# A hand-written table of steps for the work beside a state-space scan, in a fused block of scan, mixture-of-experts and attention on one Trainium2 core

## What is computed

```python
x = x + ssm(layernorm(x))        # stage 0 of the kernel, the one that the change touches
x = x + ffn(layernorm(x))        # shared experts: beside the scan; 64 routed experts: stage 1
x = x + attention(layernorm(x))  # stage 2
x = x + ffn(layernorm(x))        # stage 3

def ssm(x):                      # per batch; 16 states, rank 128
    dt_raw, b, c = split(x @ W_x.T)
    dt = softplus(dt_raw @ W_dt.T + b_dt)
    h[t] = exp(dt[t] * a) * h[t-1] + dt[t] * b[t] * x[t]     # a = -exp(A_log)
    return sum_over_states(h * c) + x * D_param

def ffn(x):
    scores = softmax(x @ gate_w.T)                 # 64 experts, the best 6, at most 64 tokens each
    y = routed experts, silu(x @ w_gate) * (x @ w_up) @ w_down, weighted by the scores
    return y + silu(x @ sw_gate) * (x @ sw_up) @ sw_down      # the shared experts
```

## Time and profile before

| | us |
|---|---|
| median of three runs | 3288.41 |
| the profiled execution, its own time | 3294.18 |
| its span | 3292.4 |
| scan stage, first to last step | 38.6 to 1144.9 |
| tail, to the first expert's work | 1145 to 1216 |
| routed experts, attention, second feed-forward | from 1216 |

### The profile page before, as it was taken

How to read it: one execution, slowest core, us unless ns; L and a number is a source line. 1 busy time by engine, 2 the same in 40 slices (tenths; PEclk the granted TensorE clock), 3 DMA queues, 4 the chain that set the end, 5 groups by cost and what they waited for, 6 DMA issues and landing times.

```text
span 3292.4 us, 38105 instructions
## 1 busy us (share of the span) xinstructions
PE 2838.2 (86%) x13772; PEld 1516.4 (46%) x13772; DVE 1785.2 (54%) x3715; ACT 1281.2 (39%) x2673; POOL 1542.7 (47%) x949
## 2 busy tenths in 40 slices
PE   4668888778888879888868999999799899999998
PEld 2445545544555434333335555555444443444443
DVE  5898897989889942212235666665324344222221
ACT  4556566555656511101116666667412121011111
POOL 6998798978879802121226555555200000212212
PEclk7669999988999989999979999999899999999999
DMA  5443453535345369999930000000234220899997
GB/s 183 141 164 129 161 187 122 191 108 191 134 161 174 134 226 339 346 344 345 330 118 1 27 27 27 27 14 14 103 112 146 93 74 21 292 350 331 345 347 196
DMA packets 199053, 557.67 MB, mean 169 GB/s; under 512 B 25040, under 2 KB 26960, under 8 KB 198352
## 3 DMA queue, kind: packets, MB, share of 16 engines
q1 hardware_dynamic: 181168, 514.19, 44.9%
q0 software_dynamic: 16640, 39.86, 5.4%
q10 hardware_dynamic: 1056, 1.18, 0.1%
HBM read 480.42 MB, written 74.74 MB: 169 GB/s over the span
## 4 chain that ended last, share of the span: by engine, by line
PE 55%; DVE 13%; POOL 12%; DMA 8%; ACT 5%; issue 4%; SPq 3%; POOLq 0%; DVEq 0%; ACTq 0%
PE bank L976 9%; PE bank L1037 7%; PE bank L943 6%; PE bank L964 6%; POOL arena L1717 6%; DMA arena<-in_w_up 4%; PE bank L1084 4%; PE bank L1141 3%; POOL arena L1723 3%; PE bank L1063 3%; PE bank L1118 3%; DVE arena L1222 3%; DVE bank L1222 2%; PE bank L885 2%; PE bank L915 2%
## 5 line engine op out<-in xcount | busy, mean ns | idle before, releaser
L1717 POOL TENSOR_TENSOR arena<-arena 128x1024 f32<-128x1024 f32 x256 | 613.2, 2396 | 90.6 <-PE bank L915 77.9
L1575 ACT ACTIVATE bank<-arena 128x512 f32<-128x512 f32 x512 | 344.1, 687 | 409.5 <-DVE arena L1222 295.5
L915 PE MATMUL bank<-arena 128*128 128x128 f32 x2048 | 308.4, 303 | 181.4 <-POOL arena L1723 181.0
L1806 POOL TENSOR_TENSOR arena<-arena 128x2048 f32<-128x2048 f32 (+3 forms) x128 | 296.8, 2321 | 277.8 <-DVE arena L1443 277.8
L915 PEld LDWEIGHTS bank<-arena 128*128 128x128 f32 x2048 | 260.2, 156 | 264.6 <-POOL arena L1723 216.0
L976 PE MATMUL bank<-arena 128*128 128x512 f32 (+1 forms) x768 | 360.5, 613 | 15.1 <-DVE arena L1245 15.1
L1638 ACT ACTIVATE arena<-arena 128x256 f32<-128x256 f32 (+3 forms) x512 | 286.2, 562 | 201.7 <-DVE arena L1434 171.5
L1222 DVE TENSOR_TENSOR_SCAN arena<-bank,arena 128x512 f32<-128x512 f32 x256 | 311.1, 1215 | 67.8 <-ACT bank L1575 45.4
L1723 POOL TENSOR_TENSOR arena<-arena 128x512 f32<-128x512 f32 x256 | 326.8, 1277 | 33.6 <-DVE arena L1222 32.9
L1037 PE MATMUL bank<-arena 128*64 128x352 f32 x2048 | 328.6, 475 | 0.0
L1222 DVE TENSOR_TENSOR_SCAN bank<-bank,arena 128x512 f32<-128x512 f32 x256 | 308.5, 1205 | 0.0
(11 more groups left out here) (134 smaller groups left out, 4196.0 us busy)
## 6 DMA issues: line engine op xcount, KB each, us to landing
arena<-scratch_bc SPq DMA_DIRECT2D x128, 1024.0 KB, 5.4
arena<-in_w_gate SPq DMA_DIRECT2D x128, 704.0 KB
arena<-in_w_up SPq DMA_DIRECT2D x128, 704.0 KB
arena<-in_w_down SPq DMA_DIRECT2D x128, 512.0 KB
arena<-in_w_down SPq DMA_DIRECT2D x128, 192.0 KB
scratch_x<-arena SPq DMA_DIRECT2D x16, 1024.0 KB, 4.5
scratch_xn<-arena SPq DMA_DIRECT2D x15, 1024.0 KB, 8.6
arena<-scratch_x SPq DMA_DIRECT2D x48, 256.0 KB, 5.9
```

What stands on the lines that cost most here:

```text
L915: i = nc.tensor.matmul(y[:, t * P:(t + 1) * P], w[:, n, t * P:(t + 1) * P], p.ident, is_transpose=True, start=False, stop=g == GROUPS - 1 ...
L1575: nc.scalar.activation(bank[p.da_bank(k, n)][:, :], block_of(p.dt, b, c), ACT.Exp, scale=p.alog[:, c, state:state + 1]).then_inc(*p.decaye ...
L1717: nc.gpsimd.tensor_tensor(out=p.hb[k % HB], in0=over(block_of(p.dtx, b, c), 1, NG), in1=p.bc[k // 2 % NBC][:, 0], op=ALU.mult).then_inc(*p ...
L1806: nc.gpsimd.tensor_tensor(out=own, in0=own, in1=over(p.rden[:, k % 2, :], 2, width), op=ALU.mult).then_inc(*p.divided.up(k))
```

## The change

`scan_plan` no longer draws pieces from generators. A table names, for each kind of thing, the step in which it stands, counted from the start of the batch beside which it begins; `prepare_track`, `quad_track` and `first_track` put the things into a list for each step. Within a step the things that take a product off its bank (`TAKERS`) come first. `route1` is cut in two, `route1` and `masks`, two steps apart. `stats` is cut in two pieces, two tiles each; for the preparation they stand in steps 7 and 8, for the front both in step 1. Picks run on into the next batch (steps 33 to 41 are 1 to 9 of it). The tail has a new table (`MADE_BESIDE`, `TAKEN_BESIDE`). No instruction's size changes; the shared experts of quad 6 end in the tail, and quad 7 begins only in stage 1, where before its first two chunks stood at the tail's end.

```diff
+PREPARE = (("x_in", 4), ("stats_a", 7), ("stats", 8), ("rstd", 8), ("apply", 11))
+FRONT = (("stats_a", 1), ("stats", 1), ("rstd", 1), ("apply", 3), ("xn_out", 3), ("gate", 7), ("logit", 9), ("route_max", 10), ("route_exp", 12), ("route1", 13), ("masks", 15))
...
+GATES, UPS = (23, 26, 29, 30, 32, 35), (23, 26, 29, 30, 33, 35)
+DOWNS = (40, 41, 43, 51)
+TURN_LAG, DT_LAG, SILU_LAG, HID_LAG, SO_LAG = 1, 2, 2, 2, 2
...
+MADE_BESIDE = {"stats": 2, "logit": 1, "pick0": 1, "pick4": 1, "merge": 1, "lists": 1}
+TAKEN_BESIDE = {"rstd": ("silu",), "apply": ("hid",), "route_exp": ("silu",), "masks": ("hid",), "pick4": ("so",),
+                "merge": ("so",), "lists": ("so",)}
...
+def quad_track(q):
+
+    f = ("F", 0, q)
+    for name, at in FRONT:
+        yield at, ((name, f) if name in ("stats_a", "stats", "rstd", "apply") else (name, 0, q))
...
+    for j in range(SC):
+        yield GATES[j], ("sg", 0, q, j)
+        yield UPS[j], ("su", 0, q, j)
+        yield GATES[j] + SILU_LAG, ("silu", 0, q, j)
+        yield UPS[j] + HID_LAG, ("hid", 0, q, j)
+    for t in range(QT):
+        yield DOWNS[t], ("fetch", 0, q, t)
+        yield DOWNS[t], ("sd", 0, q, t)
+        yield DOWNS[t] + SO_LAG, ("so", 0, q, t)
...
+TAKERS = ("turned", "dtr_out", "bc_out", "dt_out", "logit", "folded", "silu", "hid", "so")
...
-        if k <= NSTEP:
-            plan += next(coming, [])
+        if k < NSTEP:
+            plan += sorted(beside[k], key=lambda i: i[0] not in TAKERS)
         if 0 < k <= NSTEP:
-            more = next(beside, [])
-            plan += more
...
+            plan += [("sum", k - 1)]
...
-        if name == "logit":
-            plan += own[2:]
...
+        for kind in TAKEN_BESIDE.get(name, ()):
+            plan += [i for i in pending if i[0] == kind]
+            pending = [i for i in pending if i[0] != kind]
+        if name == "pick4":
+            plan += own[OUT:]
...
+    def stats_a(n):
+        sums(n, range(QT // 2))
...
     def route1(m, q):
...
         nc.vector.memset(f["top"][:, :, TOPK:], -1.0).then_inc(*p.routed.up(m, q, "six"))
+
+    def masks(m, q):
+        f, s = p.ff[m], q % 2
+        score, marked = f["score"][s], f["marked"]
         V.wait_ge(p.routed, m, q, "six")
```

More of the change, by code:

```diff
@@ L310, in scan_plan @@
                 plan += [("bc_in", k // 2 + NBC - 1)]
[L311 to L314 removed]
+        if k >= X1_BEHIND:
+            b0, c0, g0 = step_of(k - X1_BEHIND)
             if g0 == GROUPS - 1:
                 plan += [("x1", b0, c0)]
[L317 to L323 removed]
@@ new lines, in scan_plan @@
+        if 0 < k <= NSTEP:
+            plan += [("sum", k - 1)]
+    left = [i for items in beside[NSTEP:] for i in items]
+    pending = [i for i in left if i[0] in ("silu", "hid", "so") and (*PRODUCT[i[0]], *i[1:]) in plan]
+    products = [i for i in left if i[0] in ("sg", "su", "sd")]
+    own = [i for i in left if i[0] == "fetch"]
+    weights = ([("w_up", 0, e), ("w_down", 0, e)] for e in range(RING_W[0]))
+    chain = itertools.chain(front_steps(0, BATCH - 1), route_steps(0, BATCH - 1),
+                            [[("merge", 0)], [("lists", 0), ("turnover", 0)] + [("gather", 0, n) for n in range(RING_X[0])]])
@@ L354, in scan_plan @@
+    plan += own[:OUT]
+    for more in chain:
         plan += more
@@ L424, in front_plan @@
         plan += units.spend(early[0])
-        plan += [("route1", m, q)]
+        plan += [("route1", m, q), ("masks", m, q)]
         for step in coming[3:]:
@@ L1174, in stats @@
             V.wait_ge(p.xt_in[n[2] % 2], n[1], n[2])
-        for t in range(QT):
+        for t in tiles:
             if n == ("S", 0):
```

192 lines of the change are left out of this document (73 added, 119 removed).

## The result

The changed kernel takes **3191.5 us** (median of four runs, 3186.86 to 3196.82), against 3288.2 for the kernel before on the same chip: a ratio of 0.9699, 95% interval [0.9679, 0.9719]. The profiled execution takes 3196.82; its span is 3194.9 (before 3292.4), 97.5 shorter.

| | before | after | difference | forecast |
|---|---|---|---|---|
| until the last scan step starts | 1141.8 | 1040.9 | -101.0 | -44 |
| from there to the first expert matmul | 74.3 | 72.9 | -1.3 | -12 |
| to the attention's first projection | 470.6 | 479.2 | +8.6 | +1 |
| the rest | 1605.7 | 1601.9 | -3.8 | 0 |

A forecast was written before the change was run, and what follows sets the result against it. No engine was full: DVE, POOL and PE, each busy 83 to 88% in middle batches, waited in turn. Terms -43 - 1 - 12 + 1 = -55 took 3294.2 to 3239, 3233 at the median; range 3195 to 3277.

The forecast's parts named there:

- The waits go altogether: Rival, chance 0.15: in the middle batches nothing waits but DVE, 130.3 us each; with the tail -89, 3199.
- ACT's decays, 29.4: Four middle batches: DVE's 29.4 us wait for decays halves to 14.7; the part from table loads stays.
- 51.5 down to 20, 17.2 down to 9: Four middle batches: POOL's waits for `y_sum` and for DVE's scan shrink so; POOL's side sums to 533, 133.3 a batch.
- A quarter left, 5.6: Four middle batches: of DVE's 22.6 us wait for PE's products before `hid` and `so`, 5.6 stays.
- L1286's waits ... stay so: 0: Routing in the scan: DVE's product, 3.38 us mean against 0.43 with POOL idle, gains nothing.
- (a): Steps 29 and 30: `sg` and `su` in one step, 7.2 us of PE, delay `y_sum`: 0 to 2 us a batch.
- the other new waits, 0.7: Middle batches: five added costs, from paired products, `fetch`, `turned`, `dt_sum` and a logarithm table load, together 0.7 a batch.
- (e): Middle batches: one more ACT excursion to the logarithm's table, 2 x 1.28 us, costs 0 to 2 us a batch.
- First and last batch: 1 us: First and last batch, bound by POOL: `stats` in two pieces helps DVE, gaining 1 us in the first, 0 in the last.
- Sum -12: Tail, from the scan to the first expert: -11.7 for the moved `so`, -4, +2 and +1.4 give -12.
- The experts, +1: Experts' stage: two more chunks, 14.4 us of PE where 49 of 300 is free, cost 0 to 14, taken as 1.
- Slower: Rival, chance 0.05: DVE's operations with two SBUF inputs starve beside a busy POOL, up to +63, 3351.

The follow-up runs named there:

- singles_late: Changed kernel with each `su` one step behind its `sg` (`UPS` 24, 27, 30, 31, 33, 35), not paired in one step: ratio 0.9829 to the kernel before.
- places_early: Changed kernel with `sg`, `su` and `sd` at about the steps the kernel before uses, the rest of the change kept: ratio 0.9951 to the kernel before.
- places_early_lags1: Changed kernel with all products at about the old early steps and `silu`, `hid`, `so` one step behind their product, not two: ratio 0.9933 to the kernel before.
- picks_own_batch: Changed kernel with all eight picks of a pair of quads in steps 21 to 28, none in the next batch: ratio 0.9704 to the kernel before.
- routing_whole: Changed kernel with the routing uncut, `route1` and `masks` both back at step 16 instead of 13 and 15: ratio 0.9768 to the kernel before.

## Why the prediction was wrong

The direction and the mechanism were right: nothing was removed, waits went, DVE's product waits and POOL's `y_sum` waits first. The case that came was the rival "The waits go altogether", which had 0.15 and gave 3199. The waits of the middle batches went as it says, and further (127.4 us a batch, where it had 130.3); its tail did not. The middle six batches gave 97.9 us where the forecast had 43. Point by point:

- **"ACT's decays, 29.4 ... table loads ... which stay. Half left, 14.7."** This step failed: it called table loads a floor under the wait. 3.7 were left, with 64 table loads in the stretch where there had been 56. The loads were in the profile beside the wait, but they do not make it by themselves. By the rows, ACT was late because a `silu` waited for its `sg`, or for the `hid` ahead (`singles_late`), and then the two loads of 1.28 around it stood ahead of the decays. With `silu` ready in time, they fit into ACT's idle time.
- **"POOL ... with 51.5 down to 20, 17.2 down to 9."** 0.5 and 9.2 measured. The shares were set engine by engine, as if each wait was its own. The experiments show that they are not: in `places_early` DVE's wait for ACT (54.5) and POOL's for PE (47.4) are back together. Which waits show a late place depends on the place: in `singles_late` the decays are late by 20.1, POOL waits 17.4 for the scan and 0.9 for `y_sum`.
- **"A quarter left, 5.6"** of PE's 22.6: nothing was left, but nothing was left in `places_early` either (0.1), and that was 83 us slower. DVE's idle time had gone to another wait. The count of bank waits (54 to 28) is no measure of time; `places_early_lags1` has only 4 "later" ones, as the changed kernel, and is 77 us slower, of which some 4.4 us a batch are its wait for `fetch`.
- **"L1286's waits ... stay so: 0."** L1286 became 2.6 us shorter in a batch, because the change also moved the routing from step 16 to 13, where it goes at the next end of a POOL instruction. The prediction treated it as a cut only. So this step failed too: a term put at 0. DVE's busy time, taken as fixed at 505.2, fell by 10.5 (this product -10.5, `dt_sum` +5.6, a small TENSOR_SCALAR of the softmax, L1277 before, from 1314 to 264 ns each, -4.2, the comparison in `masks` +1.8, the rest -3.2). That is 10.5 of the 31.3 us by which DVE's sum was too high (541.1 forecast, 509.8 measured); ACT's term makes 11.0, PE's 5.6, POOL's releases and the short gaps 4.2.
- **"(a) ... 0 to 2 us a batch"** and the other new waits, 0.7: about right in sum. Steps 1 to 5 are 2.0 longer, but not by the last pair: in `picks_own_batch`, which keeps the pair and takes the picks out of these steps, they take 20.0 us as before. `dt_sum` costs 1.4 more in a batch, `fetch` nothing (DVE never waited for `scratch_x` in the middle batches). On (e), the cut pair of `Ln`s, the rows show what was foreseen: 8 loads more in this stretch, 10.3 us of ACT, and a wait for the decays that fell. "ScalarE: Activation LUTs" of the Trainium skill, "Table sets: the hidden batching unit", would have the sets batched; this trace shows no loss from not doing so, and no run isolates the cut.
- **First and last batch: 1 us.** 1.1 measured by the steps' starts (0.7 and 0.4). POOL bounds both. The scan also began 1.9 earlier, which is scatter: in the runs with the changed planner it begins between 36.5 and 39.2.
- **"Sum -12"** of the tail: -1.3. The 10.96 went as said. Missing was what stood ahead of the last `y_sum`s (8.00), which the order shows, and "-4" for the `sd` behind `lists` was no gain: it took 8.16 us, but beside the landing of the gather. The two are 6.9 and some 4 of the 10.7 that are missing.
- **The experts, +1.** +8.6 in this profile. In the 17 other runs with the changed planner, which leave this stage the same work, it took 464.9 to 479.0 us with a median of 474.2, one profile each, and in the two with the old one 470.6 and 469.8. So some +4 of two more chunks may be real and the rest is scatter. That was not settled.
- **"Slower", from a mean of 5.3 us** for the three DVE instructions with two SBUF inputs: the means were 3.0, 3.0 and 0.7. The mechanism exists and is worth 23 us in `routing_whole`.

The floor of 126.3 us a batch, with DVE never idle, was close to what came, 127.4, in part by luck: it was worked out with a busy time that fell, and with the one after the change, 494.7, it is 123.7. With three engines busy 83 to 88% and waits that feed each other, the forecast should have asked which places start them, and found two (steps 16 and 20 to 24, by the distances of scan starts), instead of giving each wait a share.

## What to carry to other kernels

In a loop over in-order engines, print the time of each step by its place in the period before costing anything; here a loss that the groups spread over three engines lay in a few steps. Check a hand-laid order for things that share a step with what must release them (a single buffer behind a `silu`, a bank freed behind a wait): each cost 3.5 to 4.7 us a period here, and one digit in the table was worth 38 us. A shorter lag moves more than the product's taker: here it also brought `so` too close to its `fetch`. A last wait in a tail is worth taking away only if nothing of the same length, such as a gather's landing, runs beside it.
